# A fused decoder layer: scores of two steps in a row, V parts one step earlier, norms that share a chain of roots

## The chip, the cores and the metric
The kernel runs on one core of one Trainium2 chip. The metric is device time in microseconds of one launch. TensorE (PE, with its weight loads PEld), VectorE (DVE), ScalarE (ACT), GpSimd (POOL) and the DMA queues (issued by SyncE, SP) each run their own list of instructions in order, and wait for one another by semaphores.

## The reference
32 sequences of 112 tokens by 256 features go through a decoder layer in three blocks, each followed by a layer norm. The first block is a state-space mixer with an MLP; the change doesn't touch it. The second is cross-attention to a context of 375 rows with 16 heads of 64, one key and value head for all of them, and beside it a gated MLP. The third is an MLP whose hidden values and second weights are rounded to 8-bit floats.

```python
xn = layer_norm(x, ln_g, ln_b); cn = layer_norm(context, cln_g, cln_b)
q = (xn @ Wq).reshape(b, n, 16, 64).transpose(0, 2, 1, 3) * 64 ** -0.5
k, v = jnp.split(cn @ Wkv, 2, axis=-1)
attn = softmax(jnp.einsum('bhid,bjd->bhij', q, k) + mask[:, None])
out = jnp.einsum('bhij,bjd->bhid', attn, v).transpose(0, 2, 1, 3).reshape(b, n, 1024) @ Wout
val, gate = jnp.split(xn @ W1, 2, axis=-1)
x = layernorm(x + out + silu(gate) * val @ W2)          # second block
h = float_quantize(relu(x @ w1.T + b1), 4, 3)
x = layernorm(x + float_quantize(h @ float_quantize(w2, 4, 3).T + b2, 5, 10))   # third block
```

## The kernel before, in words
The mixer runs first, for some 590 us. The rest works on 8 groups of 4 sequences (NG, GB). Everything is float32 but the last MLP's second product.

A group has 28 steps, 7 for each sequence (NP). A step computes the scores of 128 rows of (head, token) twice, for e = 0 and 1: `scores` issues one product for each, with keys and queries in 64 partitions, so that these matmuls use half of the array's height and two run side by side. In a profile each float32 product is two matmul records, so a step has four. The scores go to PSUM banks 0 and 1. Then VectorE adds the mask and takes the row maxima (`highest`, L1947), ScalarE the exponentials with their sums (`exps`, L1822), VectorE the reciprocals of the sums (`divide`, L1953), ScalarE scales (`scaled`, L1828), and VectorE turns 32 x 32 blocks (`turn`, L1961), one step behind. When the 7 steps of a sequence are turned, `times_v` multiplies the blocks by V in two parts of 48 products with 32 partitions each (L1602), a quarter of the array's height, into banks 2 to 5; ScalarE takes the result out (`heads_out`, L1836).

A step's scores may not be issued before the maxima of the step before are taken, for they share the two banks. What fills PE meanwhile are pieces of the group's other products, all with the full height of the array: queries, keys and values (kv), gate and value tiles of the gated MLP (L1627), output projections (out, L1618), transposes (back, token, ftoken), and the last MLP's up and down (L1681). A table written out by hand (`schedule`, OUT_AT, UP_AT) says in which step and slot (X or Y) each stands; another (SEAT) which of four PSUM banks it uses. Seats 2 and 3 are banks 4 and 5, which V uses too. Every engine walks the same table: in each step VectorE does `highest`, then `turn` of the step before, then norm work, then its share of the step's pieces, last `divide`; ScalarE does `scaled` of the step before, `exps`, `heads_out` where it is due, then its pieces.

Layer norms take statistics (L1205, L1208), a root by iteration (`norm_root`: L1215, L70 and three times L73, L75, L77, each waiting for the one before), and an application (L1224, on GpSimd for the tokens, the result and the final output). The context's roots go to memory and come back spread over the partitions (roots_out, roots_in), and GpSimd scales the turned context with them (L1540) ahead of kv. Each group has seven such root chains: four for contexts, one each for tokens, result and final output.

Of the kernel before, what the change touches and what calls it, by code (L numbers as in the profile page):

```python
# [10 lines left out]
ALU = mybir.AluOpType  # L11
# [4 lines left out]
J = 375  # L16
# [1036 lines left out]
RESULT, TOKENS, TOKENS_FIRST = (16, 17, 18), (20, 23, 24), (16, 17, 20)  # L1053
FINAL, FINAL_NEXT, FINAL_LAST, FINAL_AT = {STEPS - 1: (0,)}, {2: (1,)}, {STEPS - 2: (0,), STEPS - 1: (1,)}, 4
# [6 lines left out]
V_AT, V_TAKEN = (1, 2), 3  # L1061
V_BANKS = (2, 3, 4, 5)
UP_BANKS = (0, 2, 3, 4)
CONTEXT = (0, 1, 4)
# [7 lines left out]
def schedule():  # L1072

    at = {(p, s): [] for p in range(STEPS) for s in "XY"}
    at[0, "X"] += [("query", 4), ("query", 5)]
    at[1, "X"] += [("query", 6)]
    at[2, "X"] += [("query", 7)]
    at[6, "X"] += [("gate", 0)]
    at[6, "Y"] += [("value", 0)]  # L1080
    at[7, "X"] += [("gate", 1)]
    at[7, "Y"] += [("value", 1)]
    at[10, "X"] += [("gate", 2)]
    at[11, "X"] += [("value", 2)]
    at[13, "X"] += [("gate", 4)]
    at[13, "Y"] += [("back", 0), ("back", 1), ("value", 3)]
    at[14, "X"] += [("value", 4)]
    at[14, "Y"] += [("gate", 5)]
    at[15, "X"] += [("value", 5)]
    at[16, "X"] += [("gate", 6)]  # L1090
    at[17, "X"] += [("value", 6)]
    at[17, "Y"] += [("gate", 7)]
    at[18, "X"] += [("value", 7)]
    at[19, "X"] += [("ftoken", 0), ("ftoken", 1)]
    for n, p in enumerate(OUT_AT):
        at[p, "Y"].append(("out", n // KA, n % KA))
    at[11, "Y"] += [("gate", 3)]
    for n, p in enumerate(UP_AT):
        at[p, "XY"[n % 2]].append(("up", n))
    at[25, "X"] += [("token", 0), ("token", 1)]  # L1100
    at[25, "Y"] += [("down", 0)]
    at[26, "X"] += [("query", 0)]
    at[26, "Y"] += [("down", 1)]
    at[27, "X"] += [("query", 1), ("query", 2)]
    at[27, "Y"] += [("query", 3)]
    for b in range(GB):
        at[(b - 1) % GB * NP + NP - 2, "Y" if b == 3 else "X"].insert(0, ("kv", b))
    return at

def schedule_first(at):
# [4 lines left out]
    for n, piece in enumerate(tiles):  # L1116
# [20 lines left out]
SEAT = {"gate": (3, 3) + (1,) * 6, "value": (2, 2, 2) + (0,) * 5, "out": (1, 0), "kv": (2, 2, 2, 1), "query": (1, 0, 1, 2, 3, 2, 0, 0),  # L1137
        "back": (2, 3), "ftoken": (2, 3), "token": (2, 3), "down": (0, 0), "up": (0, 1) * 4}
# [88 lines left out]
def attention(nc, ctx0, PS, apart, ident, xm_dram, ctx_dram, ctx_turned, roots_dram, mask_dram, out_dram, w):  # L1227
# [3 lines left out]
    cols = sb("x_cols", [128, 8])  # L1231
    fb1 = sb("f_b1", [128, KH])
# [68 lines left out]
    x_ln = count("x_ln", LN - GB)  # L1301
# [4 lines left out]
    c_v = count("c_v", GB)  # L1306
    h_s = count("h_s", U)
# [35 lines left out]
    def vacant(eng, it, piece):  # L1343
# [41 lines left out]
    def end_bank(h, c):  # L1385
# [3 lines left out]
        return bank((7, 1)[c])[:, 0:TH]  # L1389
# [32 lines left out]
    def sync(sp, mlp):  # L1422
# [820 lines left out]
```

## Time and profile before

| | us |
|---|---|
| runs | 1777.91, 1781.38, 1781.39 (median 1781.38) |
| the profiled execution's own time | 1776.32 |
| its span, first to last instruction | 1774.5 |
| PE busy, 13256 matmul records | 1635.1 (92%) |
| DVE busy | 1301.5 (73%) |
| ACT busy | 977.7 (55%) |
| POOL busy | 578.1 (33%) |

### The profile page before, as it was taken

The page shows a single profiled execution, that of the slowest core. Times are in us where ns is not written, and L with a number is a line of the kernel's source. Part 1 is how long each engine was busy: PE and PEld are TensorE (multiplying, and loading weights), DVE is VectorE, ACT ScalarE, POOL GpSimd, SP SyncE. Part 2 cuts the span into 40 slices and gives each one's busy share as a digit, 9 for nine tenths or more (in the row PEclk, how much of TensorE's full clock was granted, in tenths as well). Part 3 has the DMA queues.
Part 4 walks back from the last instruction along what each step waited for, and adds up shares of the span by engine and source line. Part 5 has one row for each costly group of instructions (what it writes and reads, how often), then busy time and mean ns, then how long its engine had stood idle before and what let it go on. Part 6 is the DMA issues. An engine that isn't in the chain of part 4 may idle for free.

```text
span 1774.5 us, 35778 instructions
## 1 busy us (share of the span) xinstructions
PE 1635.1 (92%) x13256; PEld 957.7 (54%) x13256; DVE 1301.5 (73%) x3824; ACT 977.7 (55%) x2326; POOL 578.1 (33%) x717
## 2 busy tenths in 40 slices
PE   4579999999999978998999899899899899899897
PEld 2356676676677643454554445454454454454466
DVE  6889889889885677657767767766766776776754
ACT  3444644644632455655755755765665665665552
POOL 3878678768765101101110210210220111111101
PEclk8789999999999989999999999999999999999999
DMA  4000000010011444433333333333333333333210
GB/s 138 12 11 12 22 22 12 22 31 12 22 41 40 133 107 152 93 84 81 83 84 94 75 94 84 81 85 93 81 82 79 90 84 81 80 88 95 59 28 22
DMA packets 177614, 119.24 MB, mean 67 GB/s; under 512 B 113856, under 2 KB 171136, under 8 KB 176544
## 3 DMA queue, kind: packets, MB, share of 16 engines
q1 hardware_dynamic: 176976, 116.50, 26.5%
q8 instruction: 105, 1.72, 0.4%
q14 instruction: 69, 0.57, 0.1%
q10 hardware_dynamic: 464, 0.46, 0.1%
HBM read 96.92 MB, written 7.42 MB: 59 GB/s over the span
## 4 chain that ended last, share of the span: by engine, by line
PE 64%; DVE 17%; DMA 6%; POOL 5%; ACT 4%; issue 4%; SPq 0%; DVEq 0%; POOLq 0%; ACTq 0%
PE ps L1627 16%; PE ps L1618 10%; PE ps L1584 7%; PE ps L1602 6%; PE ps L314 4%; PE ps L387 3%; PE ps L405 3%; DVE m_u L727 3%; PE ps L1687 3%; PE ps L440 2%; DVE m_rs L759 2%; DMA x_rb<-context_roots 2%; PE ps L427 2%; POOL x_so L1224 2%; DMA context_roots<-x_st 2%
## 5 line engine op out<-in xcount | busy, mean ns | idle before, releaser
L1947 DVE CUSTOM_DVE_ANT_0 x_pr<-ps,x_mk 128x375 f32<-128x375 f32 x448 | 227.3, 544 | 212.5 <-PE ps L1584 126.1
L1828 ACT ACTIVATE x_pr<-x_pr,x_rc 128x375 f32<-128x375 f32 x448 | 247.4, 601 | 235.0 <-DVE x_rc L1953 235.0
L1540 POOL TENSOR_TENSOR x_cT<-x_cT,x_rb 128x375 f32<-128x375 f32 x64 | 57.2, 915 | 783.1 <-DMA x_rb<-context_roots 783.1
L1822 ACT ACTIVATE x_pr<-x_pr,x_mx 128x375 f32<-128x375 f32 x448 | 266.9, 597 | 80.8 <-DVE x_mx L1947 80.8
L1961 DVE STREAM_TRANSPOSE x_blk<-x_pr 128x384 f32<-128x384 f32 x448 | 231.3, 555 | 1.0 <-ACT x_pr L1828 1.0
L1627 PE MATMUL ps<-x_xn,x_w 128*128 128x448 f32 x512 | 220.5, 563 | 11.4 <-ACT x_kT L1871 3.8
L1584 PE MATMUL ps<-x_kT,x_qT 64*128 64x375 f32 x896 | 205.5, 535 | 27.4 <-DVE x_mx L1947 27.2
L1602 PE MATMUL ps<-x_blk,x_va 32*64 32x224 f32 x6144 | 163.6, 355 | 2.1 <-DVE x_ff L2004 1.7
L1602 PEld LDWEIGHTS ps<-x_blk,x_va 32*64 32x64 f32 x6144 | 133.2, 132 | 45.1 <-issue 37.8
L1627 PEld LDWEIGHTS ps<-x_xn,x_w 128*128 128x128 f32 x512 | 91.4, 192 | 118.6 <-issue 97.5
L314 PE MATMUL ps<-m_xa,w_in 128*128 128x448 f32 x352 | 148.3, 569 | 6.2 <-ACT m_xa L532 6.2
L1584 PEld LDWEIGHTS ps<-x_kT,x_qT 64*128 64x128 f32 x896 | 68.5, 187 | 156.8 <-issue 121.0
L440 PE MATMUL ps<-fc,m_gl 128*112 128x256 f32 x512 | 113.5, 380 | 0.0
L1627 PE MATMUL ps<-x_xn,x_wq 128*128 128x448 f32 x256 | 106.2, 551 | 0.0
L314 PEld LDWEIGHTS ps<-m_xa,w_in 128*128 128x128 f32 x352 | 67.5, 198 | 65.3 <-issue 56.5
L440 PEld LDWEIGHTS ps<-fc,m_gl 128*112 128x112 f32 x512 | 89.4, 177 | 20.9 <-issue 2.1
L1618 PE MATMUL ps<-x_OT,x_wo 128*128 128x448 f32 x224 | 93.6, 545 | 0.0
L1627 PE MATMUL ps<-f_xn,f_w 128*128 128x448 f32 x224 | 93.5, 555 | 0.0
L1618 PE MATMUL ps<-x_ff,x_w 128*128 128x448 f32 x224 | 90.2, 545 | 0.0
L1224 POOL TENSOR_SCALAR x_so<-x_so,x_mv,x_st 112x256 f32<-112x256 f32 x56 | 67.6, 1221 | 64.6 <-DVE x_st L77 64.6
L387 PE MATMUL ps<-m_Lm,m_R 64*16 64x64 f32 (+6 forms) x1792 | 77.0, 235 | 9.8 <-POOL m_R L1012 9.8
L427 PE MATMUL ps<-m_xb,fc 128*128 128x448 f32 x224 | 85.3, 539 | 0.0
(195 smaller groups left out, 2807.7 us busy)
## 6 DMA issues: line engine op xcount, KB each, us to landing
x_mk<-in_mask SPq DMA_DIRECT2D x224, 187.5 KB, 2.5
x_va<-x_vT SPq DMA_DIRECT2D x256, 48.0 KB, 2.1
x_cx<-in_context SPq DMA_DIRECT2D x32, 375.0 KB
x_cT<-in_context_turned SPq DMA_DIRECT2D x32, 375.0 KB, 3.5
x_rb<-context_roots SPq DMA_DIRECT2D x32, 187.5 KB, 5.1
m_Rd<-bc_roots SPq DMA_DIRECT2D x8, 448.0 KB, 3.6
x_mixed<-m_x SPq DMA_DIRECT2D x8, 448.0 KB, 3.7
X<-x_mixed SPq DMA_DIRECT2D x8, 448.0 KB, 4.5
```

The source lines that it names most:

```text
L314: last = pe.matmul(to, w_in[:, k, n * 128:(n + 1) * 128], xa[:, k, :], start=(k == 0), stop=(k == KD - 1))
L387: last = pe.matmul(bank(2 * (b % 2) + g)[0:rows, at], Rb[part, c, b, j * S:j * S + rows], Lm[part, c, b * NQ + j, :, :], start=(c == 0), s ...
L427: last = pe.matmul(bank((3, 2, 6)[n % 3])[:, 0:T], fc1[:, k, n * 128:(n + 1) * 128], xb[:, k, :], start=(k == 0), stop=(k == KD - 1))
L440: last = pe.matmul(bank(4 + b // 2)[0:S, (b % 2) * D:(b % 2 + 1) * D], gl[:, k, b * S:(b + 1) * S], fc2[:, k, :], start=(k == 0), stop=(k ...
L1584: pe.matmul(bank(e)[:, 0:J], qT[rows, b, r * ROWS:(r + 1) * ROWS], kT[rows, b % 2, :], start=True, stop=True).then_inc(h_s.sem, 1)
L1602: last = pe.matmul(bank(V_BANKS[a])[DH * e:DH * e + DH, 0:NP * BLK], va[rows, b % 2, c, :], blocks[rows, places, e, c, :], start=(c == 0), ...
L1618: last = pe.matmul(to[:, 0:T], lhs, rhs, start=(m == 0), stop=(m == KA + KH - 1))
L1627: last = pe.matmul(to[:, 0:T], weights[:, k, at:at + 128], moving[:, k, :], start=(k == 0), stop=(k == KD - 1))
L1822: act.activation(pr[:, k, 0:J], pr[:, k, 0:J], ACT.Exp, scale=-1.0, bias=mx[:, k:k + 1], accum_out=sums[:, k:k + 1]).then_inc(h_e.sem, 1)
L1828: act.activation(pr[:, k + e, 0:J], pr[:, k + e, 0:J], ACT.Copy, scale=rc[:, k + e:k + e + 1]).then_inc(h_n.sem, 1)
L1947: dve.tensor_tensor_reduce(pr[:, k + e, 0:J], bank(e)[:, 0:J], mk[:, p % SLOT, :], -1.0, 3.0e38, ALU.add, ALU.min, mx[:, k + e:k + e + 1]) ...
L1961: dve.transpose(blocks[:, place_of(p), e, :, :].rearrange("p c x -> p (c x)"), pr[:, 2 * (p % SLOT) + e, :]).then_inc(h_t.sem, 1)
```

## The change
The order of the work in the attention groups is rewritten; all the products stay.

- Scores are issued ahead. SCORED says for each of a sequence's 7 steps which scores PE issues there: none in step 0, one in step 1, those of two steps in steps 2, 4 and 6, none in 3 and 5. The pair of step 6 reaches into the next sequence. SCORE_BANKS alternates between banks 0, 1 and banks 2, 3, and each score waits for the maxima that emptied its own banks; the score of step 3 also waits until ScalarE has taken V's result out of banks 2 and 3.
- V part 0 stands at the end of step 0 and part 1 in step 1 (before: steps 1 and 2), and ScalarE takes the result in step 1 (before: 3), ahead of its pieces there.
- All filler pieces get new steps and seats.
- Roots of two norms share a chain: `context_roots` takes the variances of the context and of the tokens (last sequence of a group), the final norm (step 1) or the result (step 15) as one operand. The context's statistics are taken in step 3 of the sequence before, not in step 0.
- The result's norm is applied by VectorE in step 16, not by GpSimd in step 18.
- In the last group the output halves start two steps earlier, `end_back(0)` stands behind the other halves, and the last final norm comes in the tail.

```diff
-RESULT, TOKENS, TOKENS_FIRST = (16, 17, 18), (20, 23, 24), (16, 17, 20)
-FINAL, FINAL_NEXT, FINAL_LAST, FINAL_AT = {STEPS - 1: (0,)}, {2: (1,)}, {STEPS - 2: (0,), STEPS - 1: (1,)}, 4
+RESULT, TOKENS = (14, 15, 16), (20, 22, 23)
+FINAL = (STEPS - 1, 1, 2)
-V_AT, V_TAKEN = (1, 2), 3
+V_AT, V_TAKEN = (0, 1), 1
+SCORED = ((), (0,), (0, 1), (), (0, 1), (), (0, 1))
+SCORE_BANKS = (2, 0, 0, 2, 0, 2, 0)
-CONTEXT = (0, 1, 4)
+CONTEXT = (3, 1, 4)
...
+GATE_AT, VALUE_AT = (10, 12, 13, 15, 16, 17, 18, 19), (11, 12, 14, 16, 17, 18, 19, 20)
+UP_AT = (20, 21, 22, 23, 23, 24, 24, 25)
+QUERY_AT = (25, 26, 27, 0, 1, 2, 3, 3)
...
+    def rooted(eng, g, src, dst, done):
+        for b in range(GB):
+            eng.tensor_scalar(dst(b), src(b), mv[0:S, GB * g + b, 0:1], rt[0:S, 1, g, b:b + 1], ALU.subtract, ALU.mult).then_inc(done.sem, 1)
...
         def scores(i, p):
...
-            hold(pe, h_m, i, 2 * p)
+            k = p % NP
+            if k == 3:
+                hold(pe, o_c, i, RB * (b - 1) + 2)
+            hold(pe, h_m, i, 2 * (p - {2: 1, 3: 3}.get(k, 2)) + 2)
             for e in range(2):
                 rows = slice(DH * e, DH * e + DH)
-                pe.matmul(bank(e)[:, 0:J], ...)
+                pe.matmul(bank(SCORE_BANKS[k] + e)[:, 0:J], ...)
...
         def times_v(i, b, part):
             if part == 0:
...
+                if it < NG:
+                    pe.wait_ge(h_m.sem, h_m.value(it, 2 * p + 2))
...
         def group(it, first=False, last=False):
             for p in range(STEPS):
-                scores(it, p)
+                for ahead in SCORED[p % NP] if p or not first else (0,):
+                    if not (last and p + ahead == STEPS):
+                        scores(it + (p + ahead) // STEPS, (p + ahead) % STEPS)
...
                 parts(it, p, "X", first, last)
-                if p % NP in V_AT and (p >= NP or not first):
+                if p % NP == V_AT[1] and (p >= NP or not first):
                     i, at = back(it, p, NP)
-                    times_v(i, at // NP, V_AT.index(p % NP))
+                    times_v(i, at // NP, 1)
...
                 parts(it, p, "Y", first, last)
+                if p % NP == V_AT[0] and (p >= NP or not first):
+                    i, at = back(it, p, NP)
+                    times_v(i, at // NP, 0)
...
+        def context_roots(it, b, groups=slice(1, 2)):
+            i, k0 = held_by(it, b), CROOT * b + 2 * JT
+            v, y, t = (rt[0:JP, n, groups, :] for n in range(3))
+            dve.wait_ge(c_ln.sem, c_ln.value(i, k0))
+            dve.tensor_scalar(v, mv[0:JP, :, 1].rearrange("p (g n) -> p g n", n=GB)[:, groups, :], LN_EPS, None, ALU.add).then_inc(c_ln.sem, 1)
+            dve.wait_ge(c_ln.sem, c_ln.value(i, k0 + 1))
+            rsqrt(dve, v, y, t, c_ln, i, k0 + 1)
```

TensorE in steps 13 to 18 of a steady group, before. L1584 are scores, L1602 a V part, the others full-height pieces; numbers behind x count products.

```order
L1584 MATMUL ps<-x_kT,x_qT 128x375 x2
L1627 MATMUL ps<-x_xn,x_w_125 128x448 x2
L1649 MATMUL ps<-ident,x_oT 112x128 x8
L1627 MATMUL ps<-x_xn,x_w_125 128x448 x2
L1584 MATMUL ps<-x_kT,x_qT 128x375 x2
L1627 MATMUL ps<-x_xn,x_w_125 128x448 x4
L1584 MATMUL ps<-x_kT,x_qT 128x375 x2
L1627 MATMUL ps<-x_xn,x_w_125 128x448 x2
L1602 MATMUL ps<-x_blk,x_va 64x224 x48
L1584 MATMUL ps<-x_kT,x_qT 128x375 x2
L1627 MATMUL ps<-x_xn,x_w_125 128x448 x2
L1602 MATMUL ps<-x_blk,x_va 64x224 x48
```

And the same place now, where L1579 are scores, L1599 a V part and L1631 the result's transposes.

```order
L1579 MATMUL ps<-x_kT,x_qT 128x375 x4
L1646 MATMUL ps<-ident,x_oT 112x128 x8
L1624 MATMUL ps<-x_xn,x_w_126 128x448 x4
L1599 MATMUL ps<-x_blk,x_va 64x224 x48
L1579 MATMUL ps<-x_kT,x_qT 128x375 x2
L1624 MATMUL ps<-x_xn,x_w_126 128x448 x2
L1599 MATMUL ps<-x_blk,x_va 64x224 x48
L1579 MATMUL ps<-x_kT,x_qT 128x375 x4
L1624 MATMUL ps<-x_xn,x_w_126 128x448 x4
L1631 MATMUL ps<-ident,x_so 128x112 x8
L1624 MATMUL ps<-x_xn,x_w_126 128x448 x4
```

Runs of four score products take the place of two runs of two, and V part 0 moved ahead of the score of step 15. Over a steady group PE has 28 runs of scores before and 16 now, and changes between the three heights 64 times before and 40 now (group 0: 51 and 37).

VectorE in steps 17 and 18 before: from the turns of step 17 to those of step 18, with the result's own chain of roots.

```order
L1961 STREAM_TRANSPOSE x_blk<-x_pr 128x384 x2
L2004 TENSOR_TENSOR x_ff<-x_ff,ps 128x448
L2000 SCALAR_TENSOR_TENSOR x_ff<-x_th,ps 128x448
L1215 TENSOR_SCALAR x_st<-x_mv 112x4
L70 TENSOR_SCALAR x_st<-x_st 112x4
...
L77 SCALAR_TENSOR_TENSOR x_st<-x_st 112x4
L1953 RECIPROCAL x_rc<-x_sum 128x2
```

Now, steps 15 and 16: x_rt holds the roots of the context and of the result together (8 columns), and L1374 applies the result's norm.

```order
L1978 TENSOR_SCALAR x_rt<-x_mv 125x8
L70 TENSOR_SCALAR x_rt<-x_rt 125x8
...
L77 SCALAR_TENSOR_TENSOR x_rt<-x_rt 125x8
L2017 SCALAR_TENSOR_TENSOR x_ff<-x_th,ps 128x448
L1958 RECIPROCAL x_rc<-x_sum 128x2
...
L1966 STREAM_TRANSPOSE x_blk<-x_pr 128x384 x2
L2017 SCALAR_TENSOR_TENSOR x_ff<-x_th,ps 128x448
L2021 TENSOR_TENSOR x_ff<-x_ff,ps 128x448
L1374 TENSOR_SCALAR x_so<-x_so,x_mv,x_rt 112x256 x4
L1958 RECIPROCAL x_rc<-x_sum 128x2
```

The chain of roots of step 17 is gone, and four operations that GpSimd did stand ahead of step 16's reciprocal.

## Rows read from the trace of the kernel before

**Rows 1.** The page: busy us, share of the span, instructions.
```profile
PE 1635.1 (92%) x13256; PEld 957.7 (54%) x13256; DVE 1301.5 (73%) x3824; ACT 977.7 (55%) x2326; POOL 578.1 (33%) x717
```

**Rows 2.** Windows: length; busy by engine; granted clock; DMA share. Groups 0, 1, 5.
```profile
617.00:743.20 126.20, 104.47 (x857) 54.49 (x856) 91.47 (x326) 78.94 (x201) 17.28 (x13) 0.89 0.46 120
743.20:882.90 139.70, 134.03 (x1147) 69.38 (x1146) 96.06 (x340) 87.74 (x222) 16.76 (x16) 0.98 0.36 82
...
1302.30:1442.40 140.10, 133.78 (x1145) 69.19 (x1144) 98.07 (x351) 87.83 (x222) 21.63 (x20) 0.98 0.37 85
```

**Rows 3.** Chain of waits in group 4: start us, us, engine and line.
```profile
1188.37 1.46 PE ps L1687 x4
...
1193.66 3.20 PE ps L1627 x8
...
1198.37 0.83 PE ps L1584 x4
...
1204.74 2.46 PE ps L1602 x96
1207.20 1.70 PE ps L1618 x4
```

**Rows 4.** Timeline of PE in the tail: start us, us, line, forms, count.
```profile
1734.54 4.79 PE L1602 MATMUL ps<-x_blk,x_va 32*64 32x224 f32 x192
1739.26 0.60 PE L1744 MATMUL ps<-ident,x_xs 112*128 112x112 f32 x4
```

**Rows 5.** Timeline of PE in group 4, around steps 14 and 19.
```profile
1235.02 3.27 PE L1627 MATMUL ps<-x_xn,x_w 128*128 128x448 f32 x8 [0.52 <-DVE x_ff L2004]
...
1257.66 0.90 PE L1584 MATMUL ps<-x_kT,x_qT 64*128 64x375 f32 x4 [2.82 <-DVE x_mx L1947]
1261.38 1.76 PE L1634 MATMUL ps<-ident,x_so 112*128 112x112 f32 x8 [2.82 <-POOL x_so L1224]
1262.93 2.64 PE L1687 MATMUL ps<-x_cT,x_wkv 128*128 128x375 f32 x4
```

**Rows 6.** Window of group 4 behind the two waits (clock is third from last).
```profile
1262.90:1265.50 2.60, 2.60 (x7) 1.07 (x5) 0.00 (x0) 0.61 (x2) 0.00 (x0) 0.53 0.00 0
```

**Rows 7.** Timeline of DVE: first of a root chain, and the row behind it.
```profile
1281.49 0.13 DVE L1215 TENSOR_SCALAR x_st<-x_mv 112x4 f32<-112x4 f32 x1
...
1283.62 0.17 DVE L1953 RECIPROCAL x_rc<-x_sum 128x2 f32<-128x2 f32 x1
```

**Rows 8.** Line L1224 over the kernel: ns min/median/max.
```profile
L1224 DVE TENSOR_SCALAR x_xs<-x_xs,x_mv,x_st x8: 407/410/415, 1735.9 to 1771.3; 112x256 f32<-112x256 f32 x8
L1224 DVE TENSOR_SCALAR x_xs<-X,x_mv,x_st x4: 410/1360/1423, 584.4 to 587.3; 112x256 f32<-112x256 f32 x4
```

**Rows 9.** Timeline of all engines in one step of group 4.
```profile
1208.83 0.90 PE L1584 MATMUL ps<-x_kT,x_qT 64*128 64x375 f32 x4
...
1209.86 0.55 DVE L1947 CUSTOM_DVE_ANT_0 x_pr<-ps,x_mk 128x375 f32<-128x375 f32 x1 [0.77 <-PE ps L1584]
...
1210.80 1.03 DVE L1961 STREAM_TRANSPOSE x_blk<-x_pr 128x384 f32<-128x384 f32 x2
...
1211.78 0.17 DVE L1953 RECIPROCAL x_rc<-x_sum 128x2 f32<-128x2 f32 x1
```

**Rows 10.** Timeline of DVE: the back additions and token statistics.
```profile
1232.60 1.52 DVE L2019 TENSOR_TENSOR x_so<-ps,X 112x512 f32<-112x512 f32 x2
...
1268.96 1.36 DVE L1205 BATCH_NORM_STATS2 x_bn<-X 112x6 f32<-112x256 f32 x4
```

**Rows 11.** Timeline of ACT in step 17: taking V's result.
```profile
1251.52 1.07 ACT L1836 ACTIVATE x_OT<-ps 128x224 f32<-128x224 f32 x4
```

**Rows 12.** DMA issues: count, KB each, us to landing.
```profile
x_cT<-in_context_turned SPq DMA_DIRECT2D x32, 375.0 KB, 3.5
```

**Rows 13.** Waits from 1722 us on: total, times, longest.
```profile
DVE x_xs L2032 <- PE ps L1735: 15.0, 1, 15.0
...
PEld ps L1735 <- ACT x_oT L1900: 2.9, 1, 2.9
```

More of the change, by code:

```diff
@@ L1075, in schedule @@
     at = {(p, s): [] for p in range(STEPS) for s in "XY"}
[L1076 to L1094, printed above, removed]
+    for n, p in enumerate(QUERY_AT):
+        at[p, "X"].append(("query", n))
+    for n in range(2):
+        at[13, "X"].append(("back", n))
+        at[17, "X"].append(("ftoken", n))
+        at[24, "X"].append(("token", n))
+        at[26 + n, "Y"].append(("down", n))
     for n, p in enumerate(OUT_AT):
         at[p, "Y"].append(("out", n // KA, n % KA))
-    at[11, "Y"] += [("gate", 3)]
+    for f in range(KH):
+        at[GATE_AT[f], "X"].append(("gate", f))
+        at[VALUE_AT[f], "Y"].append(("value", f))
     for n, p in enumerate(UP_AT):
[L1099 to L1105, printed above, removed]
+        at[p, "Y" if p != 25 else "X"].append(("up", n))
     for b in range(GB):
-        at[(b - 1) % GB * NP + NP - 2, "Y" if b == 3 else "X"].insert(0, ("kv", b))
+        at[(b - 1) % GB * NP + NP - 2, "X"].insert(0, ("kv", b))
     return at
@@ L1134 @@
           + [("up", n) for n in range(KH)] + [("down", 0), ("down", 1)] + [("query", n) for n in range(QUERIES, KA)])
-SEAT = {"gate": (3, 3) + (1,) * 6, "value": (2, 2, 2) + (0,) * 5, "out": (1, 0), "kv": (2, 2, 2, 1), "query": (1, 0, 1, 2, 3, 2, 0, 0),
-        "back": (2, 3), "ftoken": (2, 3), "token": (2, 3), "down": (0, 0), "up": (0, 1) * 4}
+SEAT = {"gate": (1,) * 8, "value": (2, 3) + (0,) * 6, "out": (1, 0), "kv": (2,) * 4, "query": (1, 1, 0, 0, 0, 0, 2, 3),
+        "back": (2, 3), "ftoken": (2, 3), "token": (2, 3), "down": (3, 1), "up": (1, 0) * 4}
 def seat(piece):
@@ L1562, in gpsimd @@
                     context_scaled(it, (b + 1) % GB)
-                if p == FINAL_AT and it >= 2:
+                if p == FINAL[2] and it >= 2:
                     final_normed(it - 2)
-                if p == RESULT[2] and not first:
-                    result_normed(it - 1)
-                if p == (TOKENS_FIRST if first else TOKENS)[2] and not last:
+                if p == TOKENS[2] and not last:
                     tokens_normed(it)
@@ L1703, in group @@
                     down_token(MLP_DOWN.index(p))
-                if last and p >= STEPS - 3:
+                if last:
                     early(p)
@@ L2088, in group @@
                 parts(it, p, "Y", first, last)
-                if not first and p in RESULT[:2]:
-                    result_norm(it - 1, RESULT.index(p))
-                for stage in FINAL_NEXT.get(p, ()) if it >= 2 else ():
-                    final_norm(it - 2, stage)
-                for stage in (FINAL_LAST if last else FINAL).get(p, ()) if not first else ():
-                    final_norm(it - 1, stage)
+                if not first and p == RESULT[0]:
+                    result_norm(it - 1, 0)
+                if not first and p == RESULT[2]:
+                    result_norm(it - 1, 1)
+                if not first and not last and p == FINAL[0]:
+                    final_norm(it - 1, 0)
                 divide(it, p)
@@ L2105, in vector @@
         tokens_norm(-1, 2)
-        for stage in range(2):
-            context_norm(-1, 0, stage)
+        context_stats(-1, 0)
+        context_roots(-1, 0)
         results()
@@ L2121, in vector @@
         end_norm(0, 2)
+        for stage in range(2):
+            final_norm(NG - 2, stage)
         end_back(1)
```

126 lines of the change are left out of this document (73 added, 53 removed).

## The prediction
> **What bounds the kernel now.** I read the page's busy shares first, then the table by windows, the chain of waits, and last the timeline of one group. TensorE is busy 92% of the span, VectorE 73% [rows 1]; so TensorE is the first suspect, and the question is where its remaining time lies. Cut at the first score of each group, the windows show a steady machine: groups 1 to 6 take 139.7 to 140.1 us each, with PE busy for about 134 [rows 2]. Only group 0 (126.2 us, PE 104.5, clock 0.89) is loose. Inside a group the chain of waits is nearly all PE. The reader is to look at the lengths there [rows 3]: a step's scores take 0.83 us; eight full-height matmul records between scores 3.20, four between a V part and scores 1.70. So a record costs 0.375 us (3.20 - 1.70 = 4 x 0.375), and each such run costs 0.20 on top (3.20 - 8 x 0.375): a tenth at either end, 0.20 for each change between full-height, half-height (scores) and quarter-height (V) matmuls. The V parts say the same: two apart take 2 x 2.46 = 4.92 us, the two in a row at the kernel's end 4.72 (1734.54 to 1739.26, start to start) [rows 3, 4].
>
> Besides these changes, PE stands still at three places of a group. It idles 0.52 us in step 14 and twice 2.82 around step 19: once for VectorE's row maxima, once for GpSimd's scaled result [rows 5]. Behind the second, the granted clock is 0.53 of 2.4 GHz (nearly all at the 1.2 GHz level) [rows 6], and the four kv records take 2.64 us where they take 1.46 elsewhere [rows 5, 3]; from 1261.38 to the scores behind them PE has some 4.1 us at half speed, of which I put 1.9 down as lost (1.2 on kv, the rest on the transposes). In all 0.5 + 2.8 + 2.8 + 1.9 + 0.4 for what each wait costs beyond its idle time = 8.4 us per group. Without them a group of before would be 131.4 us.
>
> **Part 1: fewer changes of height.** By the program's order, a steady group has 28 runs of scores and 64 changes of height; the new one has 16 runs (4 of two products, 12 of four) and 40 changes. Counted over the kernel: 24 fewer in each of groups 1 to 7, 14 fewer in group 0. At 0.20 us: 4.8 us per group. Half of the 24 come from filler and V runs that join, which rows 3 and 4 show; the other half from scores that join, which no row shows: it may save nothing (0.83 us each as now) or the 0.20 of the V parts. I take 0.20, since the V parts are the nearest row and their matmuls are tiled in height as the scores are; the bound keeps 2.4 us per group.
> The Trainium skill ("TensorEngine Tiling (Array Packing)", Key Properties) says that changing the tiling mode, "not just tile", drains the engine; by it the second pair of scores, same mode, pays nothing, which is the value taken; the trace of before has no two score steps in a row without a wait to show it.
> No matmul is added, so the floor of a new group is 131.4 - 4.8 = 126.6 us.
>
> **Part 2: VectorE.** A chain of roots takes 2.13 us [rows 7]. Seven a group become four (three norms ride with the context's): 6.4 us less. The result's four scalings come over from GpSimd, at 0.41 us each or some 0.35 back to back, 1.4 us [rows 8]. Bounds: the same operation took up to 1.36 us when GpSimd worked beside it (the median of the first four) [rows 8], so 1.4 to 5.4. I take 1.4, since in step 16 GpSimd has nothing to do: its context scaling stands in step 18.
> The Trainium skill ("GPSIMD Engine Reference", Specifications) lists its SBUF interfaces as shared with VectorE; by it the move off GpSimd ends such collisions rather than making them, and the sum would stay as it is.
> VectorE is not the bound in sum, so these 5 us show only in the waits.
>
> **Part 3: the waits that go.** The score of step 19 no longer stands behind a root chain of VectorE in step 18, and the transposes of the result no longer stand behind 4.9 us of GpSimd: both 2.8 us waits go in their old form, and with them the low clock. All 8.4 us go, to be replaced as follows.
>
> **Part 4: the waits that come.** V part 0 moves to the end of step 0 and needs the last step's blocks turned. Let a pair of scores (steps 6 and 7, say) start at 0. PE: 1.45 us for four products (0.83 + 0.62), then filler F, then V. VectorE: maxima from 1.02 (1208.83 to 1209.86), 0.94 for two, turning the step before 0.95 (next 1210.80), the reciprocal not before 1.92 after the maxima's start (1211.78, behind ACT's exponentials) [rows 9]. Then 0.15, the next maxima 0.95, and the turn 0.95. So with nothing else V may start at 1.02 + 1.92 + 0.15 + 0.95 + 0.95 = 5.0; each VectorE part of the step beyond the first is added.
> - Sequence end in step 7: no parts; V is wanted at 1.45 + 4.7 = 6.15. No wait.
> - Step 14: two back additions (1.5) and a gate's product behind its tanh: VectorE at 5.15, V at 7.3; F is 4.05 us, V wanted at 5.5. Wait 1.8.
> - Step 21: token statistics (1.36 and 0.3 for their aggregates) and a value (0.55): V at 7.3 against 6.15. Wait 1.15 [rows 10].
> - Step 0 of the next group: the last down product ends at 4.9, its two additions 1.4 (as the back additions), the final statistics 1.65: divide at 8.1, V at 10.1 against 7.95. Wait 2.15 [rows 10].
>
> Queued behind each of these is all of PE; VectorE, released by nothing else, then waits for the next scores.
> The other new place is step 15 to 17. ACT takes V's output (1.07 us) in step 1 of a sequence now, ahead of the gate's tanh [rows 11]. In step 15 scores start at 0, gate 3 is done at 2.5 and V part 1 at 5.0; ACT copies until 6.25, tanh until 6.8, VectorE's product until 7.45. Gate 4 has the same seat: PE, ready at 6.5, waits 1.0. VectorE's maxima of step 16 start at 7.6; ACT scales step 15 and takes the exponentials until 10.2, then tanh; gate 4's product ends at 11.35, value 3's at 11.9, the four scalings at 13.4. PE wants to transpose the result at 10.6: wait 2.85.
> Small ones: 0.45 in steps 2 and 3 (the third score waits for two of ACT's copies, query 5 for query 4's seat), 0.1 in step 17, 0.45 in step 24, where GpSimd's token scaling ends late as it does now.
> Sum: 1.8 + 1.15 + 2.15 + 1.0 + 2.85 + 1.0 = 9.95 us per group. Each is a difference of two paths of 5 to 13 us, so I allow 4 to 14.
> The context load for the statistics, now in step 3, is issued in step 2 and lands some 4 us later (the similar loads land in 3.5 and 4.5) [rows 12]; VectorE comes to it 5 us after: hidden.
>
> **The sum.** A steady group: 139.8 - 4.8 - 8.4 + 9.95 = 136.6 us, 3.2 less; six of them -19. Last group and tail: -4.8 - 8.4, the wait for the first output halves (2.9 by its weight load) goes behind other work (-2.4) [rows 13], new waits 7.4 (no next group's tokens or statistics): -8. The last group's final norm, now in the tail, lies in VectorE's 15 us of idling there [rows 13]: nothing. Group 0: -2.8 for 14 changes; its V parts now stand ahead of scores for which VectorE waits, paired scores give as much back: -3. Together -30 us. Against the profiled execution's 1776.32 us (span 1774.5 and 1.8 around it) that is 1746; the median of the runs is 5.1 above that execution, so **1751 us**.
>
> **Rivals.**
> - Fewer waits than reckoned, about 5 us per group: the maxima are taken up to two steps ahead, and slips that I add may cover each other. 139.8 - 4.8 - 8.4 + 5 = 131.6 a group: 6 x -8.2, -4 and -12 for the ends: -65, 1716 us. Against it: ACT's order in step 15 stands in the program.
> - Scores in a row don't join (each product has its own wait): 2.4 us a group back, 139.0: -30 + 7 x 2.4 + 1.2 = -12, 1769 us. For it: only that no row shows a join.
> - The other side, the clock: in before it fell after 2.82 us of waiting, 0.9 of scores and 2.82 of waiting [rows 5, 6], once per group. The new group has four waits of 1 to 3 us at four places. If the clock falls at each for as long as now, that is 4 x 1.9 = 7.7 us a group: 144.3, 6 x +4.5, about 0 for the last and -3 for group 0: +24, 1805 us. It decides from two such falls a group on. Against it: no wait in the list stands next to a second one but those of steps 16 and 17, and the 0.52 us wait of before lowers nothing. The Trainium skill ("TensorE: Matmul & The Clock Gate", What's actually happening) has idleness as the throttled default, which only activity lifts; by it each of the four waits is a candidate and the sum would be this rival's. The trace of before bears it out at one of a group's three waits.
> - The change does its work, but the waits come to 13 us and eat it: 1776 to 1781 us, no change.
>
> **Chances.** Forecast 0.56; fewer waits 0.17; scores don't join 0.09; waits eat it 0.08; clock 0.10. Two runs of this kernel differ by about 0.2%, which is the least that counts as a change: 3.6 us. Faster: 0.56 + 0.17 + 0.09, less a bit of its tail, plus a bit of the fourth = 0.83; same 0.07; slower 0.10. The forecast's own range, waits of 7 to 12 us, is 1731 to 1766; the range takes in most of the fewer-waits case and the two small-gain ones: 1712 to 1779.
>
> **What would show it.** Right: groups 1 to 6 of 134 to 138 us; four-product rows of scores in about 1.45 us; four root chains per group; PE idle ahead of V part 0 at the end of steps 14, 21 and 0, none in step 7; an idle of some 3 us ahead of the result's transposes in step 17. Wrong: a score row of 1.66 us (no join); granted clock under 0.96 over a group (clock); PE waiting for scores' maxima again; waits under 6 or over 13 us per group.

## The result, and the profile after

The changed kernel takes 1810.0 us (median of four runs, 1804.8 to 1814.3) against 1781.3 us: a ratio of 1.0165, 95% interval 1.0135 to 1.0194. It is slower by 29 us, where 30 us less were forecast. The profiled execution took 1809.56 us, its span is 1807.7 us. Executions in the chip's slower state are left out of the ratios and of e1's median (one of its four, 1841.8 us at a mean clock of 0.916).

The page after, to compare with [rows 1]:

```profile
PE 1626.6 (90%) x13256; PEld 985.6 (55%) x13256; DVE 1281.2 (71%) x3633; ACT 982.2 (54%) x2326; POOL 543.5 (30%) x689
```

TensorE is busy 8.5 us less, though the span is 33 us longer, so it stands still more. Where, the windows tell. They are cut here at the score of step 1 of each group, which both kernels issue in its own step (the changed one issues the score of step 0 a step early, so a cut there compares unlike pieces). Columns as in [rows 2]. Before, group 0, a steady group, the last group with the tail:

```profile
617.00:748.80 131.80, 110.07 (x875) 57.03 (x874) 94.67 (x339) 83.61 (x212) 17.28 (x13) 0.90 0.46 121
1028.20:1167.90 139.70, 133.66 (x1145) 69.16 (x1144) 97.52 (x351) 87.78 (x223) 21.57 (x20) 0.98 0.36 85
1587.70:1774.50 186.80, 167.87 (x1533) 107.52 (x1532) 107.99 (x387) 91.21 (x233) 19.83 (x18) 0.97 0.22 50
```

After, groups 0, 3, 4, 5 and the last with the tail:

```profile
622.40:765.00 142.60, 107.76 (x961) 59.90 (x960) 94.23 (x328) 82.82 (x210) 17.31 (x13) 0.87 0.43 112
...
1051.40:1191.60 140.20, 130.04 (x1148) 70.65 (x1144) 93.85 (x322) 88.30 (x222) 16.80 (x16) 0.99 0.36 85
1191.60:1333.20 141.60, 131.41 (x1152) 71.19 (x1144) 93.98 (x322) 88.42 (x222) 16.79 (x16) 0.98 0.36 84
1333.20:1477.20 144.00, 133.84 (x1151) 73.10 (x1144) 93.91 (x322) 88.43 (x222) 16.79 (x16) 0.96 0.35 83
...
1621.20:1807.70 186.50, 166.24 (x1447) 110.11 (x1444) 106.94 (x369) 92.70 (x234) 15.18 (x14) 0.97 0.21 50
```

Group 0 is 10.8 us longer, groups 1 to 6 are 141.6, 144.8, 140.3, 141.6, 144.0 and 143.9 us (139.8 on the mean before), 17.3 us together, the end is the same. The other 5.4 us are ahead of the first score (617.0 and 622.4 us), in the mixer, whose code is the same.

The reader is to look at the lengths beside the clock, the third number from the end. Groups 3, 4 and 5 have the same instructions and take 140.3, 141.6 and 144.0 us. In group 3 the granted clock falls to half once, in group 4 twice, in group 5 three times, each time for 3.4 us. Group 4's last fall runs 1.0 us into group 5, so the three groups spend 3.4, 5.8 and 10.9 us at half clock. Half of that is 1.7, 2.9 and 5.4 us, and what is left is 138.6, 138.7 and 138.6 us: a fall costs 1.7 us. Taken the same way, groups 1, 2 and 6 come to 138.6 to 139.2 us. Over groups 1 to 6 there are 14 such falls; before there was one in each group, 6.8 us long, 2.8 of it during the second of the two waits [rows 5, 6].

TensorE around step 0 of group 4 and in its steps 13 to 17, after (start, us, and in brackets the idle time before and its releaser):

```profile
1183.73 1.67 PE L1615 MATMUL ps<-x_ff,x_w 128*128 128x448 f32 x4
1187.61 4.10 PE L1599 MATMUL ps<-x_blk,x_va 32*64 32x224 f32 x96 [2.21 <-DVE x_blk L1966]
...
1194.17 2.53 PE L1599 MATMUL ps<-x_blk,x_va 32*64 32x224 f32 x96
...
1250.98 3.17 PE L1624 MATMUL ps<-x_xn,x_w 128*128 128x448 f32 x8
1256.12 2.53 PE L1599 MATMUL ps<-x_blk,x_va 32*64 32x224 f32 x96 [1.96 <-DVE x_blk L1966]
...
1263.56 1.74 PE L1579 MATMUL ps<-x_kT,x_qT 64*128 64x375 f32 x8
1266.05 3.27 PE L1624 MATMUL ps<-x_xn,x_w 128*128 128x448 f32 x8 [0.75 <-DVE x_ff L2017]
1271.35 0.99 PE L1631 MATMUL ps<-ident,x_so 112*128 112x112 f32 x8 [2.03 <-DVE x_so L1374]
1272.17 4.88 PE L1624 MATMUL ps<-x_xn,x_w 128*128 128x448 f32 x8
```

V part 0 waits for turned blocks, then takes 4.03 us to the next start where its twin takes 2.46: behind the wait the clock is at half. The same shows behind the wait of 2.03 us for the result: eight records take 4.8 us, not 3.1. The two windows:

```profile
1187.50:1190.90 3.40, 3.29 (x72) 2.78 (x80) 0.17 (x1) 1.72 (x5) 0.00 (x0) 0.50 0.57 169
1272.80:1276.20 3.40, 3.40 (x6) 1.47 (x5) 2.24 (x8) 2.29 (x7) 1.71 (x2) 0.50 0.25 59
```

All 14 falls stand behind one of three waits: that of step 0 (about 140 us behind a group's cut), of step 14 (65) and of step 17 (82). None stands behind step 21, where two shorter waits (0.7 and 0.4 us) have a product between them. The same wait lowers the clock in one group and not in the next (step 14: groups 2, 5 and 6 only; step 17: all but group 3).

And TensorE's largest wait in group 0 with the two largest of VectorE there (engine, line, waited for: total, times, longest):

```profile
PE ps L1624 <- DVE x_ff L2017: 14.7, 2, 8.6
DVE x_pr L1952 <- PE ps L1579: 19.0, 6, 4.8
DVE x_bn L1193 <- DMA x_cx<-in_context: 16.5, 4, 6.0
```

Before, VectorE waited 17.4 us in this group for the scores and never for the context load. TensorE stands still for 34.7 us of group 0, where it was 21.5 before.

### The profile page after: what moved, and what is told of

It is laid out like the page before. It is cut to its first block, busy times and chain, and to the rows that moved or that the text cites. A ratio compares the mean times of both kernels' runs of the same rounds, so it can differ in the third digit from the quotient of the medians.

```text
span 1807.7 us, 35591 instructions
## 1 busy us (share of the span) xinstructions
PE 1626.6 (90%) x13256; PEld 985.6 (55%) x13256; DVE 1281.2 (71%) x3633; ACT 982.2 (54%) x2326; POOL 543.5 (30%) x689
## 4 chain that ended last, share of the span: by engine, by line
PE 64%; DVE 21%; issue 4%; DMA 4%; ACT 4%; POOL 3%; DVEq 0%; SPq 0%; POOLq 0%; ACTq 0%
PE ps L1624 15%; PE ps L1615 9%; PE ps L1599 9%; PE ps L1579 7%; PE ps L314 3%; PE ps L387 3%; PE ps L405 3%; DVE m_u L727 3%; PE ps L1684 2%; DVE x_blk L1966 2%; DVE m_rs L759 2%; PE ps L427 2%; DVE x_pr L1952 2%; PE ps L440 2%; DMA x_cx<-in_context 2%
## 5 line engine op out<-in xcount | busy, mean ns | idle before, releaser
L1624 PE MATMUL ps<-x_xn,x_w 128*128 128x448 f32 x512 | 221.7, 573 | 21.2 <-DVE x_ff L2017 20.0
L1599 PE MATMUL ps<-x_blk,x_va 32*64 32x224 f32 x6144 | 180.8, 381 | 38.3 <-DVE x_blk L1966 38.3
L1599 PEld LDWEIGHTS ps<-x_blk,x_va 32*64 32x64 f32 x6144 | 149.9, 142 | 82.6 <-issue 78.7
L1579 PE MATMUL ps<-x_kT,x_qT 64*128 64x375 f32 x896 | 183.4, 516 | 9.0 <-ACT x_qT L1854 6.1
L1624 PEld LDWEIGHTS ps<-x_xn,x_w 128*128 128x128 f32 x512 | 98.0, 200 | 122.1 <-issue 87.4
L1579 PEld LDWEIGHTS ps<-x_kT,x_qT 64*128 64x128 f32 x896 | 75.1, 188 | 105.4 <-issue 66.4
L1624 PE MATMUL ps<-x_xn,x_wq 128*128 128x448 f32 x256 | 108.6, 552 | 0.8 <-ACT x_qT L1854 0.7
L1624 PE MATMUL ps<-f_xn,f_w 128*128 128x448 f32 x224 | 93.2, 549 | 4.5 <-DVE x_ff L2021 4.5
L1374 POOL TENSOR_SCALAR x_xs<-X,x_mv,x_rt 112x256 f32<-112x256 f32 x28 | 33.8, 1220 | 182.6 <-DVE x_rt L77 182.6
```

The source lines that it names most:

```text
L1579: pe.matmul(bank(SCORE_BANKS[k] + e)[:, 0:J], qT[rows, b, r * ROWS:(r + 1) * ROWS], kT[rows, b % 2, :], start=True, stop=True).then_inc(h_ ...
L1599: last = pe.matmul(bank(V_BANKS[a])[DH * e:DH * e + DH, 0:NP * BLK], va[rows, b % 2, c, :], blocks[rows, places, e, c, :], start=(c == 0), ...
L1624: last = pe.matmul(to[:, 0:T], weights[:, k, at:at + 128], moving[:, k, :], start=(k == 0), stop=(k == KD - 1))
```

## The experiments

Beside the median and the ratio to the kernel before, each row of the table has group 0 (first score to the score of step 1 of group 1), the mean of groups 1 to 6, and the falls of the clock in these six, from each kernel's one trace.

| kernel | median us | ratio, 95% | group 0 | groups 1-6 | falls |
|---|---|---|---|---|---|
| before | 1781.3 | | 131.8 | 139.8 | 6 long |
| changed | 1810.0 | 1.0135-1.0194 | 142.7 | 142.7 | 14 |
| e1 context early | 1806.6 | 1.0109-1.0166 | 136.2 | 143.2 | 14 |
| e2 V0 in step 1 | 1766.8 | 0.9887-0.9945 | 125.9 | 137.7 | 8 |
| e3 dummy products | 1815.3 | 1.0149-1.0208 | 141.4 | 143.3 | 3 |
| e6 transposes later | 1785.7 | 1.0007-1.0042 | 139.8 | 140.1 | 9 |
| e4 = e1+e2+e6 | 1746.2 | 0.9773-0.9820 | 124.5 | 135.0 | 2 |
| e7 = e4, single scores | 1750.2 | 0.9811-0.9881 | 126.3 | 136.3 | 0 |
| e8 = e4, heads after X | 1729.7 | 0.9678-0.9744 | 125.7 | 132.7 | 2 |
| e9 = e8, seats | 1713.5 | 0.9605-0.9652 | 127.2 | 130.4 | 0 |
| e10 = e9, GpSimd | 1708.2 | 0.9567-0.9624 | 127.7 | 129.7 | 0 |
| e11 = e9, V0 back | 1753.3 | 0.9807-0.9866 | 138.1 | 135.3 | 4 |
| e12 = e9, single scores | 1726.4 | 0.9673-0.9716 | 125.4 | 132.6 | 0 |

**e1, the context load issued early** (and one load of it moved ahead of group 0).

```diff
                 if r == 2:
                     roots_out(g, n)
-                    if g + (n + 1) // GB < NG:
-                        contexts(g + (n + 1) // GB, (n + 1) % GB)
...
+                if r == 4 and it + (b + 3) // GB < NG:
+                    sp.wait_ge(c_ln.sem, c_ln.value(it + (b + 2) // GB, CROOT * ((b + 2) % GB) + 2 * JT))
+                    contexts(it + (b + 3) // GB, (b + 3) % GB)
```

> Edit on the changed kernel: SyncE issues the context load in step 4, as soon as the statistics of step 3 have read the buffer, instead of behind the roots in step 2 of the next sequence. In the changed kernel VectorE stands 54.9 us in 24 waits for this load, 16.5 of them in group 0. Theory (the load's wait is one of the causes, and a cost of group 0): these waits go, group 0 (first score to the score of step 0 of group 1, 138.3 us) shortens by 8 to 12 us, groups 1 to 7 by under 1 us each; median about 1800 us. Rival (VectorE idles there anyway, nothing waits for it): group 0 stays at 137 to 139 us, median 1808 to 1812 us.

The load's wait is gone from VectorE's list, group 0 is 6.5 us shorter (8 to 12 were expected), the steady groups are no shorter, and the median's gain of 3.4 us lies within the runs' spread. The wait shows as a cost of group 0 alone. About 1800 us were expected and did not come.

**e2, V part 0 in step 1.**

```diff
                 if p % NP == V_AT[1] and (p >= NP or not first):
                     i, at = back(it, p, NP)
+                    times_v(i, at // NP, 0)
                     times_v(i, at // NP, 1)
...
                 parts(it, p, "Y", first, last)
-                if p % NP == V_AT[0] and (p >= NP or not first):
-                    i, at = back(it, p, NP)
-                    times_v(i, at // NP, 0)
```

> Edit on the changed kernel: V part 0 stands in step 1 right ahead of part 1, behind that step's scores and its X pieces, not at the end of step 0. Theory (V part 0 asks for the turned blocks 1.5 to 2.3 us too early in steps 0, 14 and 21, and the clock falls behind two of these waits): the 4.5 us a group of waiting for turned blocks go, with them the falls some 10 and 79 us into a group, and one height change a sequence (0.8 us a group); groups of 137.4 to 144.3 us become 133.5 to 136 us, median about 1755 us. Rival (the chain of VectorE and ScalarE is the bound; the wait only moves to the next scores or seats): groups stay above 138 us, median above 1785 us.

43 us less, from one place in a sequence: 16.8 in group 0, 5.0 in each of groups 1 to 6. It stops short of the 1755 us expected, since a new wait came in its stead. The first two lines of TensorE's waits in group 4 of e2:

```profile
PE ps L1624 <- ACT x_qT L1852: 2.1, 1, 2.1
PE ps L1631 <- DVE x_so L1374: 2.0, 1, 2.0
```

The waits for turned blocks (4.5 us in three waits) are gone. TensorE comes to query 4 (L1624, in step 1) sooner and waits there for ScalarE to empty its seat. The falls that are left stand behind these two waits. The edit also joins the two V parts, so it saves changes of height (36 in a group, not 40), and the 5.0 us are not waits alone: TensorE's listed waits for other engines in group 4 go from 9.4 to 6.6 us (2.8), six falls fewer in six groups are worth 1.7, the changes of height about 1.0, and some 0.5 is lost again where rows of V products run late (last section).

**e3, products that nobody reads, ahead of V part 0.** Only work is added, and the wait for V's banks (`hold`) stands ahead of it.

```diff
+                hold(pe, o_c, i, RB * b)
+                for _ in range(2 if it < NG else 0):
+                    pe.matmul(bank(4)[:, 0:T], wq[:, 0, 0:128], wq[:, 1, 0:T], start=True, stop=True)
                 pe.wait_ge(h_t.sem, h_t.value(i, 2 * NP * (b + 1)))
```

> Edit on the changed kernel: two full-height products (128x448, 1.5 us) that nobody reads are issued ahead of every V part 0, before its wait for the turned blocks; they fill time in which TensorE otherwise stands, and shorten nothing. Theory (the clock falls because TensorE idles there): the falls some 10 and 79 us into the groups go, the one behind the result's transposes stays; a group loses 1.7 us for each fall that goes, groups 2, 5 and 6 (144.3, 143.7, 143.7) come to 140.3, the whole by 12 to 20 us less, unless step 7, where there was no wait, adds 1.5 us a group. Rival (falls aren't tied to these waits): as many falls as before (two to three a group), and the time the same or longer by up to 6 us.

Two of its groups, with and without a fall:

```profile
1052.40:1196.50 144.10, 136.60 (x1170) 73.36 (x1162) 93.91 (x322) 88.32 (x222) 16.80 (x16) 0.99 0.35 83
1196.50:1338.90 142.40, 134.91 (x1170) 72.30 (x1162) 93.91 (x322) 88.31 (x222) 16.79 (x16) 1.00 0.36 84
```

The falls of steps 0 and 14 are gone in groups 1 to 6; the three that are left stand behind the wait for the result. So it is TensorE's standing still that brings the fall, and 1.7 us is its price again. One thing was not expected: the wait for the result is 2.0 us in all six groups, as in the changed kernel, but lowers the clock in three of them, not in five. Whether a wait of this length brings a fall thus depends on something besides its own length, which no run here isolates. The 12 to 20 us expected did not come, and the rival's number did (5 us longer, within its 6), though not its reason. The products cost 1.5 us in step 7, where there was nothing to fill, and delayed the V parts in steps 0, 14 and 21 by 0.5, 0.5 and 1.1, as a part of these waits lies ahead of the dummies (for the bank, 0.85 us in step 14). That is 3.7 us a group against 3.1 for the eleven falls: no gain.

**e6, the result's transposes one slot later.**

```diff
-        at[17, "X"].append(("ftoken", n))
...
+    for n in range(2):
+        at[17, "Y"].append(("ftoken", n))
```

> Edit on the changed kernel, alone: the result's transposes one slot later (step 17 Y, behind gate 5). Theory: the wait of 2.0 to 2.2 us for the result's scaling goes, and with it the clock's fall some 82 us into a group; groups 3 to 4 us shorter (136.5 to 141 us), median 1780 to 1790 us. Rival (PE only waits at the next seat instead, since VectorE is as late there): groups shorter by under 1.5 us, median above 1798 us.

24 us less, as expected of the median, and no fall at that place any more. A group is 2.6 us shorter where 3 to 4 were expected: 1.3 of waits (9.4 to 8.1 us in TensorE's list for group 4) and 1.4 for five falls fewer. **e4** has e1, e2 and e6 together.

> Edit on the changed kernel: the early context load, V part 0 in step 1, and the result's transposes one slot later (step 17 Y, behind gate 5) together. Theory (waits that are placed one slot too early cost the change its gain): groups 1 to 6 at 130 to 133 us with at most one fall of the clock, group 0 about 125, median 1715 to 1730 us, faster than both kernels. Rival (the chain of VectorE and ScalarE bounds the group): groups of 137 to 140 us, median 1770 to 1790 us.

The three gains alone add up to 71 us; together they are 64. It is 16 us above the 1715 to 1730 expected. About that much is the new wait of e2, now alone at the start of six groups, with the two falls that are left behind it:

```profile
1149.40 0.90 PE L1583 MATMUL ps<-x_kT,x_qT 64*128 64x375 f32 x4
1152.36 1.77 PE L1628 MATMUL ps<-x_xn,x_wq 128*128 128x448 f32 x4 [2.06 <-ACT x_qT L1856]
1154.06 2.15 PE L1603 MATMUL ps<-x_blk,x_va 32*64 32x224 f32 x80
```

**e7, the pairs undone on e4.**

```diff
-SCORED = ((), (0,), (0, 1), (), (0, 1), (), (0, 1))
+SCORED = ((0,),) * NP
```

> Edit on the kernel with the three edits (1746.2 us): the pairs undone, one step's scores in each step as in the kernel before; banks, V parts and fillers stay. Theory (pairs pay by joined products, 12 joins of 0.20 us a group, and by giving VectorE its work early): groups 2.4 to 6 us longer, median 1765 to 1790 us. Rival (pairing buys nothing, the gain is all from the fillers' new order and the merged roots): within 5 us of 1746 us.

The rival's number came: 4 us, and the intervals overlap. Its reason did not hold: e7 had some 3 us a group less of waits (3.9 against 6.9 us in TensorE's list for group 5), which hid what the pairs save. e12 looks at that again with fewer waits.

**e8, ScalarE does its X pieces ahead of taking V's result.**

```diff
+                parts(it, p, "X", first, last)
                 if p % NP == V_TAKEN and (p >= NP or not first):
                     i, at = back(it, p, NP)
                     heads_out(i, at // NP)
-                parts(it, p, "X", first, last)
```

> Edit on the kernel with the three edits (1746.2 us): in step 1 of a sequence ScalarE does its X pieces (gate 3's tanh, query 4) ahead of taking V's result, not behind it. Theory (ACT's order makes the seat waits of steps 2 and 16 that I forecast at 0.45 and 1.0 us): both go, 2.1 us a group, median 1726 to 1732 us. Rival (V's result is then taken later and the score of step 3 waits for it): no gain, 1744 us or more.

2.3 us a group, as expected. TensorE's waits in step 2 and for the seat of step 16 were made by this order of ScalarE's work, as the prediction had read it in the program.

**e9, other seats, an output piece in step 0**, and **e10, the result's scalings on GpSimd.**

```diff
-OUT_AT = (0, 2, 3, 4, ...
+OUT_AT = (0, 0, 3, 4, ...
-SEAT = {..., "value": (2, 3) + (0,) * 6, ...
+SEAT = {..., "value": (3,) + (0,) * 7, ...
```

```diff
+                if p == RESULT[2] and not first:
+                    pool.wait_ge(c_ln.sem, c_ln.value(it, CROOT * GB))
+                    rooted(pool, 2, lambda b: so[:, b, :], lambda b: so[:, b, :], o_nm)
```

> Edit on the kernel with the three edits and ScalarE's new order (1729.7 us): the second output piece in step 0 instead of 2, ahead of query 4, which there waits 2.1 us for ScalarE to empty its seat; value 0 in seat 3 and value 1 in seat 0, so that kv does not wait 0.8 us for value 0's seat. Theory (these are waits for a seat and nothing behind them is late): 2 to 2.9 us a group, median 1706 to 1716 us. Rival (VectorE is late at a group's start, for the down additions and the final statistics, and V part 0 takes over the wait): 1724 us or more.

> Edit on the kernel of e9: the result's four scalings on GpSimd in step 16, as before the change, not on VectorE. A scaling takes 1.22 us there and 0.41 us on VectorE, so the result is ready 3.2 us later, but VectorE has 1.6 us less in step 16. Theory (the move to VectorE pays, since TensorE transposes the result right behind): a wait of 2 to 3 us at the transposes and a fall of the clock, 3 to 4 us a group, 20 to 30 us more than e9. Rival (the transposes now stand late enough and VectorE's relief pays for it): within 6 us of e9.

TensorE's waits in group 4 of e9, the whole list, and that group's window:

```profile
PE ps L1628 <- DVE x_ff L2023: 1.5, 2, 0.7
PE ps L1628 <- ACT x_qT L1856: 0.6, 1, 0.6
```

```profile
1140.10:1270.30 130.20, 127.89 (x1147) 70.76 (x1146) 93.10 (x324) 87.34 (x223) 16.81 (x16) 1.00 0.37 92
```

e9 is 16 us shorter than e8, within what was expected. There are 2.1 us of waiting, and the clock never falls in a steady group. In e10 a scaling takes three times as long:

```profile
L1375 POOL TENSOR_SCALAR x_so<-x_so,x_mv,x_rt x52: 1219/1223/1231, 820.8 to 1603.4; 112x256 f32<-112x256 f32 x52
```

My theory for e10 was wrong: no wait came at the transposes, which stand later than in the changed kernel. The rival's number came. e10 has the lowest median, 4% below the kernel before. The intervals of e9 and e10 overlap, but all four executions of e10 (1706.4 to 1709.2 us) lie under all four of e9 (1713.1 to 1714.8), so here the scalings are some 5 us cheaper on GpSimd.

**e11, V part 0 back at the end of step 0, all else as in e9.**

> Edit on e9 (1713.5 us): V part 0 back at the end of step 0, as in the changed kernel; all the other edits stay. Theory (this place costs the waits for turned blocks in steps 0, 14 and 21, 4.5 to 5 us a group, two falls of the clock of 1.7 us, and two fifths to one us for the height change; nothing else in the schedule makes them): groups of 129.4 to 132.2 us become 136 to 140 us, clock falls return some 5 and 65 us behind the score of step 1, group 0 grows by 8 to 15 us; median 1765 to 1785 us. Rival (the other edits have taken enough work from VectorE's path that the blocks are turned in time): groups under 134 us, median under 1745 us.

Two groups of e11, without and with a fall:

```profile
1169.40:1303.50 134.10, 128.19 (x1154) 69.95 (x1146) 93.30 (x322) 87.80 (x222) 16.82 (x16) 1.00 0.36 89
1303.50:1439.20 135.70, 129.76 (x1151) 71.12 (x1146) 93.26 (x322) 87.81 (x222) 16.81 (x16) 0.99 0.36 88
```

The one edit costs 40 us: 10.9 in group 0 and 4.8 in each of the next six. It is less than the 1765 to 1785 us expected, as 3.8 us of waiting came back and not 4.5 to 5, and only step 14's fall (four times, 1.1 us a group). The price of a fall shows a third time: 1.6 to 1.7.

**e12, single scores on e9**, with the diff of e7.

> Edit on e9 (1713.5 us): the pairs of scores undone, one step's scores in each step. On the kernel with three edits the same edit cost only 4 us, while that kernel lost about 3 us a group less in seat waits with single scores than with pairs. Theory (a join is worth 0.20 us and there are 12 a group, the seat waits hid it): with those waits gone the pairs are worth 2.4 us a group, groups of 131.5 to 134 us, median 1729 to 1738 us. Rival (joins are worth nothing, or the wait comes back elsewhere): within 6 us of e9, 1708 to 1720 us.

Group 4 of e12, to compare with the window of e9:

```profile
1143.40:1275.40 132.00, 131.40 (x1145) 68.97 (x1144) 92.92 (x323) 87.15 (x223) 16.81 (x16) 1.00 0.36 90
```

A group is 2.2 us longer and the whole 12.9 us, of which group 0 gives back 1.8. Neither number came: the theory had 1729 to 1738 us, the rival at most 1720. The 2.2 us are not the price of 12 joins, for two reasons. The waits still hide some of it: TensorE's list for group 4 is 0.6 us where e9's is 2.1. And the edit undoes joins of full-height pieces too, 24 changes of height (36 to 60), not 12. Without waits and without the delays in V's rows (0.6 and 0.5 us, last section) group 4 takes 127.6 us in e9 and 130.9 in e12: 3.4 us for 24 changes, 0.14 each, where the forecast had 0.20.

**e5, the kernel before once more.**

> The kernel before, once more, unchanged. In the profile of before the first attention score starts at 617.0 us; in the changed kernel and its three variants at 622.0 to 624.3 us, though the mixer ahead of it is the same code. Theory (one execution differs from the next by that much in the mixer): the first score comes anywhere from 617 to 624 us. Rival (the changed kernel makes the mixer slower): 617 us again, within 1 us.

Its first score came at 621.2 us. Over the traces of all kernels it came from 615.9 to 624.3 us, and the two earliest are e7 and e6, which have the changed attention groups. So the 5.4 us ahead of the first score are for the most part what one execution differs from another, and the change has no part in them that these runs could show.

## Why the prediction was wrong, point by point

**What bounds the kernel.** Right: TensorE's waits and changes of height, not VectorE's sum. Nearly all later gains came from moving waits, with the same products.

**Part 1, height changes.** Right in kind, the price somewhat too high. A row of two steps' scores takes 1.46 us in the traces, 0.20 less than 0.83 twice, as forecast; the rival "scores don't join" falls. The unwaited rest of group 4 (141.6 less 11.6 of waits and 2.9 for the clock) is 127.1 us where 126.6 was forecast, so 4.3 of the 4.8 us came; e12 gives 3.4 for as many changes.

**Part 2, VectorE.** Right in kind: it is busy 94 us a group against 97.4, 3.5 less where 5.0 were forecast, and a scaling took 0.41 us. That VectorE should have the scalings did not pay: see e10.

**Part 4, the new waits.** Nearly right. From one start to the next, less the flat length, group 4 has:

| place | forecast us | measured us |
|---|---|---|
| V part 0, step 0 | 2.15 | 2.28 |
| step 7 | 0 | 0 |
| step 14 | 1.8 | 1.93 |
| step 21 | 1.15 | 1.46 |
| seat, step 16 | 1.0 | 1.02 |
| result, step 17 | 2.85 | 2.19 |
| small ones | 1.0 | 2.7 |
| sum | 9.95 | 11.6 |

The small ones were under-counted: 1.1 us in step 2, 0.8 for value 0's seat in step 12, 0.5 in step 23, 0.2 in step 20. And step 21 came near for another reason in part: 0.9 of its 1.46 us is a wait for VectorE to empty a seat, 0.5 the wait for turned blocks.

**The step that failed: "All 8.4 us go".** In the 8.4 us stood 1.9 us for the clock, and the new waits were then counted at their idle time alone. The wait that I had seen lower the clock was 2.82 us beside another of 2.82 [rows 5, 6], and I took the single waits of 1.8 to 2.9 us for harmless, with the 0.52 us wait of before as the only witness. They are not: 14 falls in six groups, 4.0 us a group. That is two thirds of the 6.1 us by which a steady group missed (142.7 for 136.6); 1.6 are waits, 0.5 the rest. e3 takes the standing still away and 11 of the falls go; e11 brings such waits back and falls return. The clock rival, with a chance of 0.10, named the mechanism and gave 1805 us; it had four places at 1.9 us, and the chip showed three, not in every group, at 1.7. The Trainium skill ("TensorE: Matmul & The Clock Gate", What's actually happening) says that the throttled state is the default and activity releases it; by that, the trace agrees, with falls behind three of the four waits I had listed.

The clock alone did not turn the sign, though. By an estimate from the fall's price, without the 14 falls and the last group's two the kernel would take 1810 - 16 x 1.7 = 1783 us, still no gain.

**"Hidden" for the context load.** Failed. The load is issued behind the roots of step 1, and in steady groups VectorE still stands 5.2 us for it (7.3 us from issue to the statistics at 1204.36 us, where I had put 4 from other loads [rows 12]). In group 0 that is 16.5 us, and e1 gives 6.5 us of it back.

**Group 0, -3 us.** Failed by 14 us. "Paired scores give as much back" had no row behind it. Group 0 has few pieces to fill with, so with V part 0 ahead of a score, VectorE and TensorE wait in turn: TensorE stands 34.7 us there against 21.5, and 14.7 of it is for VectorE's gate products, where before the waits for x_ff came to 2.5. Moving V part 0 gave 16.8 us (e2) and putting it back took 10.9 (e11). With 6.5 for the load these cover the difference; they overlap (with the load early, the wait for gate products is 5.2 us), so their shares aren't exact.

**Last group and tail, -8 us.** It came out even (186.8 and 186.5 us): two falls (3.4), new waits of 9.1 us where 7.4 stood, and 1.0 for a wait at the down product in the tail. The rest of the miss, under 2 us, was not traced.

**The median.** The forecast went from the profiled execution; the mixer's 5.4 us are in this one's span, and some 4.5 of them not in the difference of the medians (33.2 against 28.7 us).

## What to carry to other kernels

Price a wait of the bounding engine with its idle time and with what its clock loses behind it, and take short single waits for candidates, not only long double ones. A piece that has to wait for a chain of two other engines goes behind the next work that is ready, not ahead of it: here one such move was worth 43 us, more than all the saved changes of height (some 4.8 us a group) were to bring. And where a stage has little to fill with (group 0), reckon the chain of engines by itself; the steady state's prices don't hold there.

## What the runs showed of the hardware that was not expected

In e9 the two V parts stand in a row, 192 matmul records in 4.73 us at best. In the later groups such a row takes up to 6.3 us, at the full clock and with no semaphore waited for:

```profile
1465.62 4.15 PE L1603 MATMUL ps<-x_blk,x_va 32*64 32x224 f32 x161
1470.96 1.01 PE L1603 MATMUL ps<-x_blk,x_va 32*64 32x224 f32 x31 [1.19 <-issue]
```

TensorE stands 1.19 us in the middle of the row for nothing that the profile names. The rows grow like this, with gaps of the same kind, in e2, e4, e7, e8, e10 and e12 too (in e7 and e12 also in groups 1 and 2, up to 6.5 us). Rows of 96 with a filler or scores between them stay at 2.46 us; of those at full clock in groups 1 to 6 of the changed kernel two took longer, by 0.2 and 0.4 us. What holds the engine up is open. The load on the DMA queues alone is not it, as the same row of group 1 and of group 6 shows (the DMA share is the last number but one):

```profile
814.80:819.50 4.70, 4.70 (x192) 4.40 (x192) 4.54 (x21) 2.92 (x9) 0.00 (x0) 1.00 0.88 253
1465.60:1471.90 6.30, 5.09 (x192) 4.36 (x192) 5.93 (x28) 2.94 (x9) 0.00 (x0) 1.00 0.52 147
```

It costs up to 1.6 us a row and is the larger part of why groups 5 and 6 of e9 (130.8 and 132.2 us) are longer than group 1 (129.4).
